# State products of 102 columns in two PSUM banks, and a new order of VectorE's work behind the norm

## The reference, cut to what matters

```python
# attention, 16 heads of 16; q and k with rope, then elu(.) + 1
kv = kv + einsum('bhd,bhm->bhdm', kt, vt)      # state, token by token
ks = ks + kt
out_t = einsum('bhd,bhdm->bhm', qt, kv) / maximum(einsum('bhd,bhd->bh', qt, ks), 1e-6)
x = x + out @ w_out
# experts: 8, all computed, gate and up 256 -> 256, down 256 -> 256
h = silu(einsum('btd,edi->beti', x, Wg)) * einsum('btd,edi->beti', x, Wu)
out = einsum('bte,betd->btd', weights, einsum('beti,eid->betd', h, Wd))
x = x + out
```

## Time and profile before

| what | value |
|---|---|
| median of 3 runs | 796.18 us (794.05 to 797.39) |
| profiled execution | 795.6 us, of which span 793.8 us |
| mean granted TensorE clock | 0.991 |
| PE / PEld busy | 97% / 84% |
| DVE / ACT / POOL busy | 77% / 59% / 61% |
| ordinary step, routing step | 22.52 us, 23.88 us (starts of the same PE work in the timeline) |

### The profile page before, as it was taken

One profiled execution on the slowest core, in us unless ns is written; L12 is line 12 of the kernel. 1 busy time (PEld: TensorE's weight loads), 2 busy tenths in 40 slices (PEclk: granted clock), 3 DMA queues, 4 the chain that ended last, 5 costly groups with the idle time before them and its releaser, 6 DMA issues.

```text
span 793.8 us, 18445 instructions
## 1 busy us (share of the span) xinstructions
PE 772.2 (97%) x6864; PEld 668.2 (84%) x6864; DVE 607.7 (77%) x1565; ACT 466.3 (59%) x886; POOL 481.9 (61%) x537
## 2 busy tenths in 40 slices
PE   9778899999999999999999999999999999999998
PEld 8666788888888888888888888888888888888887
DVE  7898877879777797778877797788877788756343
ACT  5665776656656656565666566657656666634222
POOL 4886667756566576655666656566676655653322
PEclk9999999999999999999999999999999999999999
DMA  6635331122211031222201221120111121100000
GB/s 171 147 81 111 79 68 47 41 43 68 42 40 29 17 68 41 41 44 65 41 15 31 43 67 42 41 43 19 51 42 41 40 54 28 28 2 27 1 1 26
DMA packets 97320, 38.28 MB, mean 48 GB/s; under 512 B 74192, under 2 KB 96976, under 8 KB 97232
## 3 DMA queue, kind: packets, MB, share of 16 engines
q1 hardware_dynamic: 90704, 30.83, 18.0%
q10 hardware_dynamic: 6528, 6.29, 2.7%
HBM read 16.13 MB, written 4.19 MB: 26 GB/s over the span
## 4 chain that ended last, share of the span: by engine, by line
PE 86%; DVE 6%; POOL 2%; ACT 2%; DMA 2%; issue 2%; SPq 0%; ACTq 0%; DVEq 0%; POOLq 0%
PE y L478 21%; PE up L444 21%; PE gate L444 21%; PE front L304 5%; PE front L305 3%; PE back L356 3%; PE back L400 2%; PE up L375 2%; PE up L412 1%; PE front L327 1%; DMA qT<-q_st 1%; PE back L344 1%; PE front L425 1%; PE back L327 1%; PE y L275 1%
## 5 line engine op out<-in xcount | busy, mean ns | idle before, releaser
L1230 POOL TENSOR_TENSOR h_lo<-work,h_hi 128x512 fp32r<-128x512 f32 x126 | 163.3, 1296 | 63.8 <-ACT h_hi L683 63.0
L1201 POOL TENSOR_TENSOR a_lo<-am,a_hi 128x512 f16<-128x512 f32 x120 | 142.2, 1186 | 52.1 <-ACT a_hi L610 49.6
L478 PE MATMUL y<-wd_hi,h_hi 128*128 128x256 f32 x504 | 145.9, 289 | 0.0
L478 PE MATMUL y<-wd_lo,h_hi 128*128 128x256 f32 x504 | 140.6, 279 | 0.0
L478 PE MATMUL y<-wd_hi,h_lo 128*128 128x256 f32 x504 | 140.4, 278 | 0.0
L1069 DVE TENSOR_TENSOR work<-work,up 128x512 f32<-128x512 f32 x128 | 86.9, 679 | 62.9 <-PE up L444 62.8
L683 ACT ACTIVATE h_hi<-work 128x512 fp32r<-128x512 f32 x126 | 79.3, 629 | 60.6 <-DVE work L1069 33.7
L1085 DVE SCALAR_TENSOR_TENSOR xa<-y,wo,xa 128x256 f32<-128x256 f32 x252 | 111.5, 470 | 2.0 <-PE y L478 2.0
L610 ACT ACTIVATE a_hi<-am 128x512 f16<-128x512 f32 x120 | 74.7, 625 | 41.9 <-DVE am L847 38.3
L478 PEld LDWEIGHTS y<-wd_hi,h_hi 128*128 128x128 f32 x504 | 94.7, 188 | 4.2 <-issue 0.2
L478 PEld LDWEIGHTS y<-wd_lo,h_hi 128*128 128x128 f32 x504 | 94.9, 188 | 2.7
(11 more groups left out here) (227 smaller groups left out, 1773.8 us busy)
## 6 DMA issues: line engine op xcount, KB each, us to landing
xr<-xT SPq DMA_DIRECT2D x32, 128.0 KB, 2.5
xa<-x SPq DMA_DIRECT2D x32, 128.0 KB, 2.5
out<-xa SPq DMA_DIRECT2D x32, 128.0 KB, 1.7
xa<-Wg ACTq DMA_DIRECT2D x8, 256.0 KB, 2.7
work<-Wd ACTq DMA_DIRECT2D x8, 256.0 KB, 3.3
work<-Wu ACTq DMA_DIRECT2D x8, 256.0 KB, 2.9
work<-w_qkv SPq DMA_DIRECT2D x2, 384.0 KB, 3.6
kT<-k_st SPq DMA_TRANSPOSE x32, 3.1
```

Source lines behind the costliest of these rows:

```text
L478: m = pe.matmul(y_bank(n, t), h_at(hi, n)[:, t * P:(t + 1) * P], wd_p[wi][:, u // KI, u % KI, :], start=(n % KI == 0 and (t % 2 == 0 or n ...
L1201: pool.tensor_tensor(a_p[1][:, heads(r), :], am_place(g, r).rearrange("p (h n) -> p h n", h=4), a_p[0][:, heads(r), :], ALU.subtract).then ...
L1230: pool.tensor_tensor(h_at(1, n), hb[:, n % 2, :], h_at(0, n).bitcast(F32), ALU.subtract).then_inc(s_hlo, 1)
```

## The change

From tile 8 on (`PARTS = 8`) the state product runs as 8 matmuls of 102 columns: a pair's three value parts side by side (3 parts x 2 heads x 17 columns). The three sums are no longer made in PSUM. 5 pairs go to U and 3 to R1. The R1 part stands inside `av(c)`, between the masked products and `from_state`. VectorE adds each part to its own running sum `st_p` (three sums, in the space of the former staging buffer), with two instructions for U (`st_add`, 255 columns) and two for R1 (`st_add_r1`, 153 columns). GpSimd adds the three sums to `st_s` (`st_sum`, two instructions of 136 columns), and `s1` waits for that. `st_parts` clears and fills `st_p` once, in step 8. VectorE's order behind the norm is new, and on ScalarE `fb` goes behind `v_copy`.

```diff
             def scores(g, half):
+                if g > PARTS:
+                    w.wait_ge(s_ssr, 2 * (g - PARTS))
+            def state_parts(g, bank, first, last, done):
+                if bank is R1:
+                    w.wait_ge(s_v, tiles(g + 1))
+                for p in range(first, last):
+                    m = pe.matmul(bank[:, (p - first) * 2 * WV:(p - first + 1) * 2 * WV],
+                                  k_st[:, g % 2, 2 * p:2 * p + 2, :, :].rearrange("p h c d -> p (h c d)"),
+                                  vx[:, g % 2, 2 * p:2 * p + 2, :, :].rearrange("p h s d -> p (h s d)"),
+                                  start=(p == first), stop=(p == last - 1), skip_group_check=True)
+                m.then_inc(done, 1)
             def av(g):
+                if g >= PARTS:
+                    state_parts(g, R1, NPU, NP, s_stater)
                 if g >= NT:
                     from_state(False, True)
             def state(g):
+                if g >= PARTS:
+                    state_parts(g, U, 0, NPU, s_state)
+                    return
...
-                th(router); qk_copy(a); fb(router); v_copy(a); e1(router); exp(a); silu(n + 1)
+                th(router); qk_copy(a); v_copy(a); fb(router); e1(router); exp(a); silu(n + 1)
...
+            def parts_add(bank, first, last, done):
+                new = bank[:, 0:(last - first) * 2 * WV].rearrange("p (q h s d) -> p q h s d", q=last - first, h=2, s=3)
+                for hh in range(2):
+                    rows = slice(64 * hh, 64 * hh + 64)
+                    v.scalar_tensor_tensor(out=st_p[rows, first:last, :, :], in0=new[rows, :, hh, :, :], scalar=ASCALE,
+                                           in1=st_p[rows, first:last, :, :], op0=ALU.mult, op1=ALU.add).then_inc(done, 1)
+            def st_parts(g):
+                if g != PARTS - 1:
+                    return
+                v.memset(st_p[:, :, 1:3, :], 0.0).then_inc(s_stp, 1)
+                v.tensor_copy(st_p[:, :, 0, :], st_s[:, :, :]).then_inc(s_stp, 1)
+            def st_add_r1(g):
+                w.wait_ge(s_stater, g - PARTS + 1)
+                parts_add(R1, NPU, NP, s_ssr)
...
-                route_first(router); norm(c); route_second(router); q_lo(a); k_lo(a); o_lo(c); h_up(n + 1)
+                route_first(router); norm(c); st_add_r1(c); h_up(n + 1); st_parts(c); q_lo(a); o_lo(c); k_lo(a); route_second(router)
                 route_tie(router); x1_add(c); acc(n - 2, 0); bn2(c); route_ix2(router); acc(n - 2, 1)
...
+            def st_sum(g):
+                w.wait_ge(s_ss, 2 * g + 2)
+                w.wait_ge(s_ssr, 2 * (g - PARTS) + 2)
+                pool.tensor_tensor(st_s[:, :, :], st_p[:, :, 0, :], st_p[:, :, 1, :], ALU.add).then_inc(s_sum1, 1)
+                w.wait_ge(s_sum1, g - PARTS + 1)
+                pool.tensor_tensor(st_s[:, :, :], st_s[:, :, :], st_p[:, :, 2, :], ALU.add).then_inc(s_sum, 1)
...
-                v_rest(a); h_lo(n); h_lo(n + 1); rstd2_pow(c); st_rest(c)
+                st_sum(c); v_rest(a); h_lo(n); h_lo(n + 1); rstd2_pow(c); st_rest(c)
```

More of the change, by code:

```diff
@@ L43 @@
 LAST = UNITS * NB - 4
+PARTS = 8
+NPU = 5
 def bcast(ap, axis, n):
@@ L143, in build @@
         hb, stage = work[:, 0:2, :], work[:, 2:4, :]
+        st_p = stage[:, 0, 0:NP * WV].rearrange("p (q s d) -> p q s d", q=NP, s=3)
         h_p = [sb(f"h_{s}", [P, 2, B], F32R) for s in ("hi", "lo")]
@@ L169, in build @@
              "slab_hi", "slab_lo"))
-        (s_qkv, s_qk, s_av, s_state, s_oT, s_proj, s_x2T, s_lgrows, s_logit, s_gate, s_up, s_down, s_last) = (
+        (s_qkv, s_qk, s_av, s_state, s_oT, s_proj, s_x2T, s_lgrows, s_logit, s_gate, s_up, s_down, s_last, s_stater) = (
             sem(n) for n in ("qkv", "scores", "av", "state", "o_T", "proj", "x2_T", "logit_rows", "logit", "gate", "up",
-                             "down", "down_last"))
+                             "down", "down_last", "state_r1"))
         (s_xhi, s_qkc, s_v, s_exp, s_qhi, s_khi, s_v1, s_v2, s_ahi, s_s1, s_s2, s_ohi, s_lgc, s_th, s_e1, s_fb,
@@ L180, in build @@
         (s_slab_lov, s_xlo, s_bn, s_mv, s_ve, s_cos, s_rope, s_phi, s_qlo, s_klo, s_amask, s_o, s_ss, s_den, s_rec, s_norm, s_olo, s_x1,
-         s_bn2, s_mv2, s_ve2, s_x2n, s_x2lo, s_h, s_acc, s_hlov) = (sem(n) for n in (
+         s_bn2, s_mv2, s_ve2, s_x2n, s_x2lo, s_h, s_acc, s_hlov, s_stp, s_ssr) = (sem(n) for n in (
              "slab_lo_v", "x_lo", "bn", "mv", "ve", "cos", "rope", "phi", "q_lo", "k_lo", "masked", "o", "ss", "den", "rec", "norm",
-             "o_lo", "x1", "bn2", "mv2", "ve2", "x2n", "x2_lo", "h", "acc", "h_lo_v"))
+             "o_lo", "x1", "bn2", "mv2", "ve2", "x2n", "x2_lo", "h", "acc", "h_lo_v", "state_parts", "ss_r1"))
         ROUTE = ("sum", "inh", "off", "zone", "dist", "zone2", "m", "eq", "w0", "c", "ws", "ix", "no", "s1", "nd",
@@ L186, in build @@
         s_route = sem("router_step")
-        s_rstd1, s_sin, s_vr, s_v3, s_alo, s_sr, s_s3, s_rstd2, s_hlo = (sem(n) for n in (
-            "rstd1", "sin", "vr", "v3", "a_lo", "sr", "s3", "rstd2", "h_lo"))
+        s_rstd1, s_sin, s_vr, s_v3, s_alo, s_sr, s_s3, s_rstd2, s_hlo, s_sum1, s_sum = (sem(n) for n in (
+            "rstd1", "sin", "vr", "v3", "a_lo", "sr", "s3", "rstd2", "h_lo", "st_sum1", "st_sum"))
         def routed(b, step):
@@ L618, in s1 @@
                 w.wait_ge(s_ss, 2 * g + 2)
+                if g >= PARTS:
+                    w.wait_ge(s_sum, g - PARTS + 1)
                 act.activation(st_x[:, :, 0, :], st_s[:, :, :], ACT.Copy).then_inc(s_s1, 1)
@@ L875, in st_add @@
                 w.wait_ge(s_state, g + 1)
+                if g >= PARTS:
+                    w.wait_ge(s_stp, 2)
+                    w.wait_ge(s_sum, g - PARTS)
+                    parts_add(U, 0, NPU, s_ss)
+                    return
                 stp = state_bank(g)[:, 0:NP * 2 * W1].rearrange("p (q h d) -> p q h d", q=NP, h=2)
@@ L880, in st_add @@
                                            op0=ALU.mult, op1=ALU.add).then_inc(s_ss, 1)
+            def st_parts(g):
+                if g != PARTS - 1:
+                    return
+                for n in range(SLABS - NSL, SLABS):
+                    w.wait_ge(*slab_lo_done(n))
+                w.wait_ge(s_ss, 2 * PARTS)
+                v.memset(st_p[:, :, 1:3, :], 0.0).then_inc(s_stp, 1)
+                v.tensor_copy(st_p[:, :, 0, :], st_s[:, :, :]).then_inc(s_stp, 1)
+            def st_add_r1(g):
+                if not live(g) or g < PARTS:
+                    return
+                w.wait_ge(s_stp, 2)
+                w.wait_ge(s_sum, g - PARTS)
+                w.wait_ge(s_stater, g - PARTS + 1)
+                parts_add(R1, NPU, NP, s_ssr)
             def den_max(g):
@@ L1202, in a_lo @@
                                    a_p[0][:, heads(r), :], ALU.subtract).then_inc(s_alo, 1)
+            def st_sum(g):
+                if not live(g) or g < PARTS:
+                    return
+                w.wait_ge(s_ss, 2 * g + 2)
+                w.wait_ge(s_ssr, 2 * (g - PARTS) + 2)
+                w.wait_ge(s_s1, g)
+                w.wait_ge(s_sr, g)
+                pool.tensor_tensor(st_s[:, :, :], st_p[:, :, 0, :], st_p[:, :, 1, :], ALU.add).then_inc(s_sum1, 1)
+                w.wait_ge(s_sum1, g - PARTS + 1)
+                pool.tensor_tensor(st_s[:, :, :], st_s[:, :, :], st_p[:, :, 2, :], ALU.add).then_inc(s_sum, 1)
             def st_rest(g):
```

## The result

The changed kernel takes 800.76 us (median of 6 runs, 799.81 to 802.69), the kernel before 795.66 us (median of 6, 794.05 to 797.39). The ratio is 1.0065, with a 95% interval of 1.0049 to 1.0082: slower by 5.1 us. The forecast was 802.0 us, in a range of 792.0 to 804.5. The difference is under 1%, but the whole interval lies above 1: it is slower.

What follows compares the result with a forecast made beforehand. TensorE, busy 97% of the span, was taken as the bound. Ordinary steps -4.3 us and routing steps +10.2 gave +5.9 on 795.6, so 801.5; the median, 0.6 higher, made it 802.0, range 792.0 to 804.5.

Steps and rivals of the forecast that it cites:

- The wide matmuls: TensorE's state product: 46 ns per 102-column matmul, 0.37 us for eight instead of 0.61, saving 0.24 us a tile.
- The sums on VectorE: VectorE, every step: 0.90 us on U and 0.70 on R1, 1.0 us more a step, hidden in ordinary steps.
- GpSimd's sums: `st_sum` ahead of `v_rest`: two instructions of about 0.45 us, done at about 460.8, hidden with little to spare.
- The holds: Routing steps: L1011 and L1013 wait on VectorE for two GpSimd `h_lo`, making `x1_add` 1.7 us late.
- No slack behind `x1_add`: Routing steps: 0.05 us between `acc(n - 2, 3)` and TensorE's third token tile of `down(n)`, so delay passes on.
- Sum: Whole kernel: 18 ordinary steps give -4.3 us and six routing steps +10.2, together +5.9 us.
- the skill's price: State matmuls at about 65 ns for 102 columns, 0.52 us for eight: only 0.09 us a tile saved.
- rival C: Holds plus ordinary steps that give nothing (wide matmuls 0.52 us or `o_lo` late): 805 to 806 us, chance 0.11.

Runs made afterwards that it cites:

- Experiments 1: The kernel before with only VectorE's new order behind the norm, without wide state matmuls or added sums: 804.67 us, ratio 1.0113.
- 2: The changed kernel with `route_second` back in its old place right behind the norm: 801.19 us, ratio 1.0072.
- 3: The changed kernel with five routing instructions that read two SBUF tensors replaced by reciprocals reading one, from the second block on: 795.72 us, ratio 0.9991.
- 5: The changed kernel with `silu(n + 2)` ahead of `h_hi(n + 1)` on ScalarE, VectorE's list untouched: 795.63 us, ratio 1.0000.

## Why the prediction was right

The mechanism was right, not only the number: two holds in six routing steps, less a small saving in 18 ordinary ones.

- The wide matmuls: forecast 46 ns each and 0.24 us a tile, measured 48 ns and 0.22. The bounds had been wide, and the rows of f16 with 128 columns decided rightly. The Trainium skill's 81 ns at 128 columns ("TensorE: Matmul & The Clock Gate", Back-to-back issue gap) would have given, as an estimate scaled with the columns, 65 at 102; this trace does not agree with it.
- The sums on VectorE: forecast 0.90 us for the two on U and 0.70 for the two on R1, measured 0.87 and 0.65. Hidden in ordinary steps, as forecast: three of them are shorter by 0.53 to 0.66 us, 0.2 each, and TensorE's weight loads wait for `o_lo` 4.6 us in all, where they waited 4.8. That the ordinary steps gave the forecast -4.3 us in all is partly luck: 0.6 of it is the wait for k's transpose, which nobody had counted on, and without it they gave -3.7.
- GpSimd's sums ended at 463.57 and `v_rest` followed at 463.58. ScalarE's `v1` had ended at 463.06 + 0.44 = 463.50. The forecast had the sums end 0.16 us ahead of `v1` (460.8 against 460.52 + 0.44); they ended 0.07 behind it, so `v_rest` was late by that much.
- The holds: forecast 0.75 us for L1011's successor and 1.3 for L1013's, each ending with an `h_lo`, and `x1_add` 1.7 us late; measured 0.82, 1.22 and 1.70. Experiments 1, 2, 3 and 5 show the mechanism from four sides: the order alone brings it, other instructions in that place get it, one input less removes it, and a gap on GpSimd removes half.
- No slack behind `x1_add`: forecast 0.05 us. The routing steps grew by 1.66 us. The prediction looked at the third token tile of `down(n)` alone and expected six waits there; TensorE waits twice in each routing step, and the first token tile, with 0.46 us of slack before, takes 1.18 of the 1.39 us that its matmuls wait.
- Sum: forecast +5.9 us, measured +5.1 between medians and +5.3 between the profiled executions: +10.0 for the routing steps (forecast +10.2), -4.3 for the others, +0.2 ahead of the loop and -0.6 at the end. The last two were in no forecast.
- One slip that changed nothing: "3.6 us higher" for the skill's price counts 24 tiles, while the sum counts 18, which would be 2.7, as rival C has it.

The rule of the Trainium skill ("SBUF — State Buffer", SBUF: two separate sides) that a VectorE instruction with two SBUF inputs and a GpSimd instruction that reads SBUF need the same port pair, under a lock held for a whole instruction, agrees with the rows here: 0.82 and 1.22 us held, 0.19 free, and reciprocals with one input at 0.34 inside an `h_lo`.

Three of my own experiments' sizes were off: the order alone (10.6 expected, 9.0 measured), the reciprocals (10 and 5.0), and a little the one hold (6 and 5.1).

## What to carry to other kernels

Before small work is moved into a busy place, look at what the other engines do there. A 0.19 us instruction that reads two SBUF tensors took up to 1.22 us beside a long GpSimd instruction, and a 0.17 us tensor_scalar with one took 0.61; reductions, reciprocals and instructions with one of two inputs in PSUM were not held in the rows above. And GpSimd may stand there only because the same move made its input ready earlier. Look for work whose result is needed late, and move that out of the chain with no slack; here that turned a loss of 5.1 us into a gain of 5.1. An experiment that moves a stall to the next instruction of the same kind (2) says more on the cause than one that just removes it.

## What was not expected of the hardware

A reciprocal of 32 elements a partition took 0.34 us, one of 16 elements 0.24 and one of 4 elements 0.18, while a tensor_tensor of 32 elements took 0.19: the reciprocal's time grew with its size in this range.

A tensor_scalar with a single tensor input was held by GpSimd, as said at experiment 3. No run here tries what else it depends on.

And the same 45 us of TensorE's expert work near the end took 44.65 us in the profiled execution of the kernel before (738.36 to 783.01) and 44.03 to 44.15 in those of all eight other kernels, two of which differ from it only in VectorE's order. The granted clock was 1.00 there in both the kernel before and the changed one. So that half a microsecond belongs to one execution and not to the change. Nothing here explains it; it is as large as a tenth of the effect measured.
